# A fused adaptive feed-forward kernel on one core: the last tile's mean taken from the matmuls as a product with the weights' row sums, with the weights kept in rows of 528 elements

## The chip, the cores and the metric

The kernel runs on one core of a Trainium2 chip. The metric is device time in microseconds (us) of one execution, the median over runs of the same kernel. The engines are TensorE (PE; its weight loads are PEld), VectorE (DVE), ScalarE (ACT), GpSimd (POOL) and SyncE (SP), which issues most DMAs. Each runs its own list of instructions in order, and they wait for one another by semaphores.

## The reference

64 sequences of 32 tokens with 512 features, all float32. A small network turns each sequence's condition into a 32 x 32 mixing matrix and a bias; the mixed tokens go through a feed-forward network with a shared and a routed part, whose sum is normalised over the features and added to x.

```python
h = einsum('boi,bih->boh', agg_w, x) + agg_b[:, :, None]      # agg_w, agg_b from the condition
logits = h @ gate_w;  w = top_k(logits, 2)[0].sum(-1)
shared = relu(h @ up_w) ** 2 @ down_w                          # 512 -> 1024 -> 512
routed = ((h @ fc1_w) @ expert_w) * w @ fc2_w                  # 512 -> 256 -> 256 -> 512
y = shared + routed
out = x + (y - y.mean(-1)) * rsqrt(y.var(-1) + 1e-5) * gamma + beta
```

## The kernel before

The 2048 tokens are 16 tiles of 128 tokens, four tiles to a block, so there are four blocks: block 0 is written out, blocks 1 and 2 are one loop body, block 3 is written out. Products are made in float32 precision from operands split into a high and a low part (`down_hi`, `down_lo`, ...): `three_products` issues high x high, high x low and low x high, three matmuls with one destination in PSUM. The expert matrix is folded into fc2 ahead of time, which gives `q` (256 x 512).

In a block TensorE runs the up product (eight chunks `m` of 128 columns of up_w, twelve matmuls each, in four PSUM banks that are reused in turn), the latent and gate products, the mixing for the next block, and the down product. The down product goes tile by tile: six matmuls with `q`, 24 with `down`, each with 512 columns. The bank for up chunk m is free when ScalarE's relu of chunk m - 4 has read it (`relu_done`), and that relu waits until VectorE has split chunk m - 2 (`sq_lo_ready`), because `relu_sq` has two buffers. In the down product tile t waits for VectorE's first sum of tile t - 2 (`y_done`).

VectorE's `normalise(b, t)` adds the two products, takes statistics (L714, L717), adds epsilon (L719), subtracts the mean and multiplies by gamma (L721), waits for GpSimd's `rstd` (a power of -0.5, L417), and makes the result with `x_beta` (L727), which SP stores. GpSimd computes `x_beta` for the next block (L410) once the last tile of a block is finished, and copies the next mixing tiles (L405) after VectorE's reduction of them (L656). VectorE then splits the squares of the next block (L685 a cast, L687 a subtraction).

The last tile of the last block is different. The routing weight is multiplied into its latents beforehand, so that both products add up in one PSUM group, and its 512 columns are made in two halves of 30 matmuls with 256 columns each, in two banks. `normalise_last` takes statistics of each half (L739), aggregates them (L746), and then makes each half's product with gamma (L749) and result (L757). The epsilon is put into the first half's statistics (L742).

The order of all instructions is the order in the code; nothing reorders them. The rows of `down_hi`, `down_lo`, `q_hi` and `q_lo` are 512 float32 elements (2048 bytes) in each partition, and the matmul operands lie in SBUF one behind the other, each tensor starting at a multiple of 128 bytes.

## Time and profile before

| | |
|---|---|
| median of 3 runs | 256.64 us |
| the 3 runs | 256.37, 256.64, 646.71 us |
| profiled execution: span from first to last instruction | 254.6 us |
| median less the span | 2.0 us |
| TensorE busy, granted clock (mean) | 97%, 0.995 |
| VectorE, ScalarE, GpSimd busy | 61%, 32%, 15% |
| chain that ended last | TensorE 89%, DMA 3%, issue 2% |
| last matmul's end to the end of the span | 249.62 to 254.6 us |

The profiled execution's own device time is not listed apart from its span; the 2.0 us stand for what lies around the span. The busy shares are averages over the whole span. Which engine sets the time is read from the chain and from the timeline of each stage: where TensorE is without a gap, what other engines do costs nothing, and after its last matmul every microsecond on the chain of the others is paid.

### The profile page before, as it was taken

Reading aid. Unit: us, or ns where it says so; the run is one execution under the profiler, and the core shown is the slowest. Engines: PE = TensorE matmul, PEld = TensorE weight load, DVE = VectorE, ACT = ScalarE, POOL = GpSimd, SP = SyncE. Lnnn points to the kernel's source line nnn. Section 1 sums busy time; section 2 is a strip of 40 time slices with the busy share of each in tenths; the row PEclk is TensorE's granted clock in tenths of the full one; section 3 lists DMA queues with packets and bytes.
Section 4 is the critical chain, followed back from the end, with each engine's and each line's share of the span. In section 5 each row is a group of like instructions: output and inputs, shape, how many; then the busy total and the mean of one; then the engine's idle time right before and its main releaser. Section 6 shows DMA issues by size and latency. Waiting matters only on the chain.

```text
span 254.6 us, 3526 instructions
## 1 busy us (share of the span) xinstructions
PE 248.0 (97%) x1291; PEld 207.1 (81%) x1291; DVE 155.8 (61%) x272; ACT 81.8 (32%) x142; POOL 39.4 (15%) x45
## 2 busy tenths in 40 slices
PE   8999999999999999999999999999999999999992
PEld 7877887988888888888888888888888888788891
DVE  4798999944448964644447983464444953406453
ACT  4669856411003452321112534331111355202100
POOL 2400021000117120001114411001111700001110
PEclk9999999999999999999999999999999999999997
DMA  6994804001111400001111220000011100000111
GB/s 161 332 324 153 305 17 153 0 0 44 41 41 41 167 0 0 3 0 42 41 41 41 78 87 0 0 0 11 31 41 44 42 0 0 0 3 8 74 44 41
DMA packets 10444, 15.60 MB, mean 61 GB/s; under 512 B 1088, under 2 KB 4928, under 8 KB 10432
## 3 DMA queue, kind: packets, MB, share of 16 engines
q1 hardware_dynamic: 9984, 15.33, 17.6%
q8 instruction: 8, 0.13, 0.2%
q10 hardware_dynamic: 448, 0.11, 0.2%
q14 instruction: 4, 0.03, 0.0%
HBM read 11.23 MB, written 4.20 MB: 61 GB/s over the span
## 4 chain that ended last, share of the span: by engine, by line
PE 89%; DMA 3%; issue 2%; DVE 1%; SPq 1%; ACT 0%; POOL 0%; POOLq 0%; DVEq 0%
PE ps L932 27%; PE ps L934 27%; PE ps L933 27%; PE ps L906 4%; DMA late<-in_up_w_dram 3%; PE ps L998 2%; PE ps L950 1%; PE ps L956 1%; PE ps L952 1%; SPq L322 0%; POOL rstd L417 0%; DVE stats L714 0%; DVE y_buf L712 0%; DVE h_full L636 0%; ACT h_hi L474 0%
## 5 line engine op out<-in xcount | busy, mean ns | idle before, releaser
L932 PE MATMUL ps<-down_hi,sq_hi 128*128 128x512 f32 (+1 forms) x136 | 51.2, 377 | 0.0
L933 PE MATMUL ps<-down_lo,sq_hi 128*128 128x512 f32 (+1 forms) x136 | 51.2, 377 | 0.0
L934 PE MATMUL ps<-down_hi,sq_lo 128*128 128x512 f32 (+1 forms) x136 | 51.2, 376 | 0.0
L932 PE MATMUL ps<-h_hi,up_hi 128*128 128x512 f32 x120 | 46.8, 390 | 0.0
L934 PE MATMUL ps<-h_hi,up_lo 128*128 128x512 f32 x120 | 46.7, 389 | 0.0
L933 PE MATMUL ps<-h_lo,up_hi 128*128 128x512 f32 x120 | 46.7, 389 | 0.0
L417 POOL TENSOR_TENSOR rstd<-mv,half 128x1 f32<-128x1 f32 x16 | 15.3, 954 | 158.2 <-DVE mv L719 153.2
L512 ACT ACTIVATE relu_sq<-ps 128x512 f32<-128x512 f32 x32 | 19.1, 597 | 57.7 <-PE ps L934 44.3
L712 DVE TENSOR_TENSOR y_buf<-ps,y_buf 128x512 f32<-128x512 f32 x15 | 10.4, 692 | 41.0 <-PE ps L934 40.7
L685 DVE CAST sq_hi<-relu_sq 128x512 fp32r<-128x512 f32 x32 | 22.6, 706 | 16.2 <-ACT relu_sq L514 15.7
L932 PEld LDWEIGHTS ps<-down_hi,sq_hi 128*128 128x128 f32 x136 | 25.6, 188 | 4.7
L933 PEld LDWEIGHTS ps<-down_lo,sq_hi 128*128 128x128 f32 x136 | 25.6, 188 | 4.7
L934 PEld LDWEIGHTS ps<-down_hi,sq_lo 128*128 128x128 f32 x136 | 25.6, 188 | 4.7
L529 ACT ACTIVATE y_buf<-ps,top 128x512 f32<-128x512 f32 x15 | 10.2, 687 | 56.7 <-PE ps L934 56.7
L687 DVE TENSOR_TENSOR sq_lo<-relu_sq,sq_hi 128x512 fp32r<-128x512 f32 x32 | 26.5, 828 | 1.1
L932 PEld LDWEIGHTS ps<-h_hi,up_hi 128*128 128x128 f32 x120 | 22.5, 188 | 5.0 <-DVE up_lo L619 0.4
L934 PEld LDWEIGHTS ps<-h_hi,up_lo 128*128 128x128 f32 x120 | 22.5, 188 | 4.7
L933 PEld LDWEIGHTS ps<-h_lo,up_hi 128*128 128x128 f32 x120 | 22.5, 188 | 4.6
L514 ACT ACTIVATE relu_sq<-relu_sq 128x512 f32<-128x512 f32 x32 | 20.2, 632 | 1.0
L727 DVE SCALAR_TENSOR_TENSOR late<-y_buf,rstd,late 128x512 f32<-128x512 f32 x15 | 11.3, 752 | 7.6 <-POOL rstd L417 5.6
L410 POOL TENSOR_TENSOR late<-x_cur,affine_sb 128x2048 f32<-128x2048 f32 x3 | 14.2, 4750 | 2.8 <-DVE late L727 2.8
L932 PE MATMUL ps<-q_hi,lat_hi 128*128 128x512 f32 (+1 forms) x34 | 13.3, 390 | 0.0
(137 smaller groups left out, 308.7 us busy)
## 6 DMA issues: line engine op xcount, KB each, us to landing
out_dram<-late SPq DMA_DIRECT2D x15, 256.0 KB, 2.0
x_cur<-in_x_dram SPq DMA_DIRECT2D x3, 1024.0 KB, 5.2
late<-in_down_w_dram SPq DMA_DIRECT2D x4, 512.0 KB, 5.3
late<-in_up_w_dram SPq DMA_DIRECT2D x3, 512.0 KB, 8.8
x_cur<-in_x_dram SPq DMA_DIRECT2D x2, 512.0 KB, 7.2
experts_sb<-in_experts_dram SPq DMA_DIRECT2D x3, 256.0 KB, 3.5
agg_b<-aggb_dram SPq DMA_DIRECT2D x1, 768.0 KB, 4.9
latents_sb<-in_latents_dram SPq DMA_DIRECT2D x1, 528.0 KB, 4.8
```

Of the source, the lines that this page charges most:

```text
L410: nc.gpsimd.tensor_tensor(x_beta, x_cur[:, :, :], beta_b.unsqueeze(1).to_broadcast([P, TB, HID]), ALU.add).then_inc(xbeta_ready, 1)
L417: nc.gpsimd.tensor_tensor(rstd[:, :], mv[:, 1:2], half[:, :], ALU.pow).then_inc(rstd_done, 1)
L512: nc.scalar.activation(relu_sq[:, m % 2, :], ps[:, UP_BANK[m], :], ACT.Relu).then_inc(relu_done, 1)
L514: nc.scalar.activation(relu_sq[:, m % 2, :], relu_sq[:, m % 2, :], ACT.Square).then_inc(square_done, 1)
L529: nc.scalar.mul(y_buf[:, t % 2, :], routed(t), top2[:, t:t + 1]).then_inc(scaled_done, 1)
L685: nc.vector.tensor_copy(sq_hi[:, m, :], relu_sq[:, m % 2, :]).then_inc(sq_hi_ready, 1)
L687: nc.vector.tensor_tensor(sq_lo[:, m, :], relu_sq[:, m % 2, :], sq_hi[:, m, :].bitcast(fp32), ALU.subtract).then_inc(sq_lo_ready, 1)
L712: nc.vector.tensor_tensor(y, shared(t), y, ALU.add).then_inc(y_done, 1)
L727: nc.vector.scalar_tensor_tensor(out=out_buf[:, t, :], in0=y, scalar=rstd[:, :], in1=x_beta[:, t, :], op0=ALU.mult, op1=ALU.add).then_inc( ...
L932: nc.tensor.matmul(dst, a_hi, b_hi, start=first, stop=False)
L933: nc.tensor.matmul(dst, a_hi, b_lo, start=False, stop=False)
L934: return nc.tensor.matmul(dst, a_lo, b_hi, start=False, stop=last)
```

## The change

The normalisation's mean of a token is the sum of its 512 outputs over 512, and that sum is the product of the token's activations with the row sums of the weights. So two equal columns (512 and 513) are added behind the 512 of `down_hi`, `down_lo`, `q_hi` and `q_lo`; they hold the rows' sums, split in high and low. Rows become 528 elements long (2112 bytes). The sums are made once by VectorE, between the normalisations of block 0's tiles: one reduction behind tile 0, one behind tile 1, and two behind tile 2 with five small instructions that add the parts and split them. In the last tile, the half with columns 256 to 511 is now made first, with columns 512 and 513 after it in the same matmuls (258 columns), so column 256 of its PSUM bank holds the tile's sum when it is done. `normalise_last` divides it by 512 (`last_mean`) and makes the first half's product with gamma while TensorE works at the second half. The other half's product follows the aggregation and no longer waits for its mean. TensorE's last tile waits for `sums_ready`. SP stores the halves in the new order.

```diff
 
         up_hi = sb("up_hi", [P, HC, INT], f32r)
         up_lo = sb("up_lo", [P, HC, INT], f32r)
-        down_hi = sb("down_hi", [P, IC, HID], f32r)
-        down_lo = sb("down_lo", [P, IC, HID], f32r)
+        down_hi = sb("down_hi", [P, IC, HID + PAD], f32r)
+        down_lo = sb("down_lo", [P, IC, HID + PAD], f32r)
         fc1_hi = sb("fc1_hi", [P, HC, LAT], f32r)
         fc1_lo = sb("fc1_lo", [P, HC, LAT], f32r)
-        q_hi = sb("q_hi", [P, LC, HID], f32r)
-        q_lo = sb("q_lo", [P, LC, HID], f32r)
+        q_hi = sb("q_hi", [P, LC, HID + PAD], f32r)
+        q_lo = sb("q_lo", [P, LC, HID + PAD], f32r)
 
 
         h_hi = sb("h_hi", [P, HC, TOK], f32r)
...
         ones = sq_lo[:, 1, 0:P]
         half = sb("half", [P, 1])
         warm = sb("warm", [P, 1])
+        row_sums = sb("row_sums", [P, 2, IC + LC])
+        last_mean = sb("last_mean", [P, 1])
 
         ps = ctx.enter_context(nc.psum_tensor("ps", [P, 8, TOK], fp32))
         H1 = ps[:, 4, 0:2 * NB].rearrange("p (a b) -> p a b", a=2)
...
         def routed(t):
             return ps[:, 6 + t % 2, :]
 
+        LAST_COLS = [slice(HID // 2, HID + 2), slice(0, HID // 2)]
+
         def last_shared(half):
 
             return [shared(TB - 1), ps[:, LAT_BANK[0], :]][half][:, 0:HID // 2]
+
+        LAST_MEAN = shared(TB - 1)[:, HID // 2:HID // 2 + 1]
 
 
         mlp_loaded = [sem(f"mlp_loaded{i}") for i in range(2)]
...
                 store_block(b)
             store_block(NBLK - 1, TB - 1)
             for half in (0, 1):
-                cols = slice(half * HID // 2, (half + 1) * HID // 2)
+                cols = [slice(HID // 2, HID), slice(0, HID // 2)][half]
                 sp.wait_ge(final_done, NT + half)
                 sp.dma_start(out_v[:, NT - 1:NT, cols], out_buf[:, TB - 1:TB, cols]).then_inc(stored[TB - 1], 16)
             for t in range(TB - 1):
...
             def down_high(i):
                 ks = slice(i * DNC, (i + 1) * DNC)
                 act.wait_ge(down_loaded[i], 16)
-                nc.scalar.copy(down_hi[:, ks, :], down_raw[:, ks, :]).then_inc(down_hi_ready, 1)
+                nc.scalar.copy(down_hi[:, ks, 0:HID], down_raw[:, ks, :]).then_inc(down_hi_ready, 1)
 
             for m in range(IC):
                 relu_square(0, m)
...
                                                in1=x_beta[:, t, :], op0=ALU.mult,
                                                op1=ALU.add).then_inc(final_done, 1)
 
+            def sum_rows(weights, at, n, part):
+                nc.vector.tensor_reduce(row_sums[:, part, at:at + n], weights[:, :, 0:HID].bitcast(fp32), AX.X,
+                                        ALU.add).then_inc([hi_summed, lo_summed][part], 1)
+
+            def split_sums():
+                dve.wait_ge(hi_summed, 2)
+                dve.wait_ge(lo_summed, 2)
+                nc.vector.tensor_tensor(row_sums[:, 0, :], row_sums[:, 0, :], row_sums[:, 1, :], ALU.add
+                                        ).then_inc(rows_summed, 1)
+                dve.wait_ge(rows_summed, 1)
+                nc.vector.tensor_copy(down_hi[:, :, HID:HID + 2], row_sums[:, 0, 0:IC].unsqueeze(2).to_broadcast([P, IC, 2])
+                                      ).then_inc(sum_hi_ready, 1)
+                nc.vector.tensor_copy(q_hi[:, :, HID:HID + 2], row_sums[:, 0, IC:IC + LC].unsqueeze(2).to_broadcast([P, LC, 2])
+                                      ).then_inc(sum_hi_ready, 1)
+                dve.wait_ge(sum_hi_ready, 2)
+                nc.vector.tensor_tensor(down_lo[:, :, HID:HID + 2], row_sums[:, 0, 0:IC].unsqueeze(2).to_broadcast([P, IC, 2]),
+                                        down_hi[:, :, HID:HID + 2].bitcast(fp32), ALU.subtract).then_inc(sums_ready, 1)
+                nc.vector.tensor_tensor(q_lo[:, :, HID:HID + 2], row_sums[:, 0, IC:IC + LC].unsqueeze(2).to_broadcast([P, LC, 2]),
+                                        q_hi[:, :, HID:HID + 2].bitcast(fp32), ALU.subtract).then_inc(sums_ready, 2)
+
             def normalise_last():
 
                 b, t = NBLK - 1, TB - 1
                 n = NT
                 y = y_buf[:, t % 2, :]
-                halves = [slice(0, HID // 2), slice(HID // 2, HID)]
+                halves = [slice(HID // 2, HID), slice(0, HID // 2)]
+
+                def times_gamma(i):
+                    cols = halves[i]
+                    nc.vector.scalar_tensor_tensor(out=y[:, cols], in0=last_shared(i), scalar=last_mean[:, :],
+                                                   in1=gamma_b[:, cols], op0=ALU.subtract,
+                                                   op1=ALU.mult).then_inc(gamma_done, 1)
+
                 for i, cols in enumerate(halves):
                     dve.wait_ge(shared_done, n + i)
                     nc.vector.bn_stats(out=last_stats[:, i, :], in_=last_shared(i)).then_inc(stats_done, 1)
...
                         dve.wait_ge(stats_done, n)
                         nc.vector.tensor_scalar(last_stats[:, 0, 2:3], last_stats[:, 0, 2:3], HID * EPS, None,
                                                 ALU.add).then_inc(eps_added, 1)
+                        nc.vector.tensor_scalar(last_mean[:, :], LAST_MEAN, 1.0 / HID, None,
+                                                ALU.mult).then_inc(last_mean_ready, 1)
+                        dve.wait_ge(last_mean_ready, 1)
+                        times_gamma(0)
                 dve.wait_ge(eps_added, 1)
                 dve.wait_ge(stats_done, n + 1)
                 nc.vector.bn_aggr(out=mv[:, :], in_=last_stats[:, :, :]).then_inc(mv_done, 2)
-                dve.wait_ge(mv_done, 2 * n)
-                for i, cols in enumerate(halves):
-                    nc.vector.scalar_tensor_tensor(out=y[:, cols], in0=last_shared(i), scalar=mv[:, 0:1],
-                                                   in1=gamma_b[:, cols], op0=ALU.subtract,
-                                                   op1=ALU.mult).then_inc(gamma_done, 1)
+                times_gamma(1)
                 dve.wait_ge(gamma_done, n + 1)
                 dve.wait_ge(rstd_done, n)
                 dve.wait_ge(xbeta_ready, b + 1)
...
             mix_bias(1, 3)
             mix_low(1, 2)
             mix_low(1, 3)
-            for t in range(TB):
-                normalise(0, t)
+            normalise(0, 0)
+            sum_rows(down_hi, 0, IC, 0)
+            normalise(0, 1)
+            sum_rows(down_lo, 0, IC, 1)
+            normalise(0, 2)
+            sum_rows(q_hi, IC, LC, 0)
+            sum_rows(q_lo, IC, LC, 1)
+            split_sums()
+            normalise(0, 3)
             with dve.Fori(1, NBLK - 1) as b:
                 for m in range(IC):
                     split_square(b, m)
...
                         pe.wait_ge(h_ready, HC * b + 3)
                     if last_block and t == TB - 1:
                         pe.wait_ge(last_lo_ready, LC)
+                        pe.wait_ge(sums_ready, 3)
                         for half in (0, 1):
-                            cols = slice(half * HID // 2, (half + 1) * HID // 2)
+                            cols = LAST_COLS[half]
+                            dst = [shared(TB - 1)[:, 0:HID // 2 + 2], last_shared(1)][half]
                             for lc in range(LC):
-                                three_products(last_shared(half), lat_hi[:, lc, rows], lat_lo[:, lc, rows],
+                                three_products(dst, lat_hi[:, lc, rows], lat_lo[:, lc, rows],
                                                q_hi[:, lc, cols], q_lo[:, lc, cols], lc == 0, False)
                             for m in range(IC):
-                                last = three_products(last_shared(half), sq_hi[:, m, rows], sq_lo[:, m, rows],
+                                last = three_products(dst, sq_hi[:, m, rows], sq_lo[:, m, rows],
                                                       down_hi[:, m, cols], down_lo[:, m, cols],
                                                       False, m == IC - 1)
                             last.then_inc(shared_done, 1)
...
                             pe.wait_ge(lat_hi_ready, LC * b + lc + 1)
                             pe.wait_ge(lat_lo_ready, LC * b + lc + 1)
                         last = three_products(routed(t), lat_hi[:, lc, rows], lat_lo[:, lc, rows],
-                                              q_hi[:, lc, :], q_lo[:, lc, :], lc == 0, lc == LC - 1)
+                                              q_hi[:, lc, 0:HID], q_lo[:, lc, 0:HID], lc == 0, lc == LC - 1)
                     last.then_inc(routed_done, 1)
                     for m in range(IC):
                         if t == 0:
```

The parts left out are the new semaphores and the same `0:HID` in other places that write or read these tensors.

VectorE, block 0, before: the end of tile 2's normalisation and the start of tile 3's. `late` holds the results and `x_beta`.

```order
L727 SCALAR_TENSOR_TENSOR late<-y_buf,rstd,late 128x512
L712 TENSOR_TENSOR y_buf<-ps,y_buf 128x512
L714 BN_STATS stats<-y_buf 128x6
L717 BN_AGGR mv<-stats 128x2
L719 TENSOR_SCALAR mv<-mv 128x1
```

VectorE at the same place now, from the end of tile 2's normalisation on:

```order
L740 SCALAR_TENSOR_TENSOR late<-y_buf,rstd,late 128x512
L745 TENSOR_REDUCE row_sums<-q_hi 128x2
L745 TENSOR_REDUCE row_sums<-q_lo 128x2
L751 TENSOR_TENSOR row_sums<-row_sums 128x10
L754 CAST down_hi<-row_sums 128x8x2
L756 CAST q_hi<-row_sums 128x2x2
L759 TENSOR_TENSOR down_lo<-row_sums,down_hi 128x8x2
L761 TENSOR_TENSOR q_lo<-row_sums,q_hi 128x2x2
L725 TENSOR_TENSOR y_buf<-ps,y_buf 128x512
L727 BN_STATS stats<-y_buf 128x6
```

Two reductions, a sum, two casts and two subtractions stand between tiles 2 and 3. Between tiles 0 and 1 and between tiles 1 and 2 stands one reduction of `down_hi` and of `down_lo` (eight rows of 512 elements each to 128x8).

VectorE, the last tile, before; `last_stats` are the statistics, `y_buf` the product with gamma, `late` the result:

```order
L739 BN_STATS last_stats<-ps 128x6
L742 TENSOR_SCALAR last_stats<-last_stats 128x1
L739 BN_STATS last_stats<-ps 128x6
L746 BN_AGGR mv<-last_stats 128x2
L749 SCALAR_TENSOR_TENSOR y_buf<-ps,mv,affine_sb 128x256 x2
L757 SCALAR_TENSOR_TENSOR late<-y_buf,rstd,late 128x256 x2
```

and now:

```order
L779 BN_STATS last_stats<-ps 128x6
L782 TENSOR_SCALAR last_stats<-last_stats 128x1
L784 TENSOR_SCALAR last_mean<-ps 128x1
L773 SCALAR_TENSOR_TENSOR y_buf<-ps,last_mean,affine_sb 128x256
L779 BN_STATS last_stats<-ps 128x6
L790 BN_AGGR mv<-last_stats 128x2
L773 SCALAR_TENSOR_TENSOR y_buf<-ps,last_mean,affine_sb 128x256
L797 SCALAR_TENSOR_TENSOR late<-y_buf,rstd,late 128x256 x2
```

One product with gamma has moved ahead of the second half's statistics, with a one-element scaling of the sum ahead of it; one has stayed behind the aggregation.

TensorE, the step from tile 2 of the last block to the first half of the last tile, before:

```order
L934 MATMUL ps<-down_hi,sq_lo 128x512
L932 MATMUL ps<-q_hi,lat_hi 128x256
L933 MATMUL ps<-q_lo,lat_hi 128x256
L934 MATMUL ps<-q_hi,lat_lo 128x256
L932 MATMUL ps<-q_hi,lat_hi 128x256
```

and now:

```order
L981 MATMUL ps<-down_hi,sq_lo 128x512
L979 MATMUL ps<-q_hi,lat_hi 128x258
L980 MATMUL ps<-q_lo,lat_hi 128x258
L981 MATMUL ps<-q_hi,lat_lo 128x258
L979 MATMUL ps<-q_hi,lat_hi 128x258
```

The 30 matmuls of this half have 258 columns for 256; the second half's 30 keep 256. The number of instructions on TensorE is the same.

## Rows read from the trace of the kernel before

**Rows 1.** The page: busy times (1) and the granted clock in 40 slices (2)

```profile
PE 248.0 (97%) x1291; PEld 207.1 (81%) x1291; DVE 155.8 (61%) x272; ACT 81.8 (32%) x142; POOL 39.4 (15%) x45
...
PEclk9999999999999999999999999999999999999997
```

**Rows 2.** Timeline, TensorE, last tile: start us, length us, line, operation, count

```profile
242.27 0.28 PE L932 MATMUL ps<-q_hi,lat_hi 128*128 128x256 f32 x1
...
249.34 0.28 PE L934 MATMUL ps<-down_hi,sq_lo 128*128 128x256 f32 x1
```

**Rows 3.** Table by stretch, one tile of block 0: stretch, its length, busy (count)

```profile
54.73:61.53 6.80, 6.80 (x32) 5.63 (x31) 3.14 (x7) 0.69 (x1) 0.92 (x1) 1.00 0.11 41
```

**Rows 4.** Timeline, VectorE, the end of the program

```profile
246.26 0.43 DVE L739 BATCH_NORM_STATS2 last_stats<-ps 128x6 f32<-128x256 f32 x1
...
249.66 0.43 DVE L739 BATCH_NORM_STATS2 last_stats<-ps 128x6 f32<-128x256 f32 x1 [2.79 <-PE ps L934]
250.22 0.21 DVE L746 BATCH_NORM_AGGREGATE mv<-last_stats 128x2 f32<-128x12 f32 x1
250.47 0.88 DVE L749 SCALAR_TENSOR_TENSOR y_buf<-ps,mv,affine_sb 128x256 f32<-128x256 f32 x2
251.38 0.88 DVE L757 SCALAR_TENSOR_TENSOR late<-y_buf,rstd,late 128x256 f32<-128x256 f32 x2
```

**Rows 5.** Timeline, GpSimd, the end of the program

```profile
250.51 0.55 POOL L417 TENSOR_TENSOR rstd<-mv,half 128x1 f32<-128x1 f32 x1 [5.01 <-DVE mv L746]
```

**Rows 6.** Timeline, VectorE and GpSimd, an ordinary tile of the last block

```profile
232.45 0.74 DVE L721 SCALAR_TENSOR_TENSOR y_buf<-y_buf,mv,affine_sb 128x512 f32<-128x512 f32 x1
...
232.61 0.98 POOL L417 TENSOR_TENSOR rstd<-mv,half 128x1 f32<-128x1 f32 x1 [30.26 <-DVE mv L719]
...
233.69 0.75 DVE L727 SCALAR_TENSOR_TENSOR late<-y_buf,rstd,late 128x512 f32<-128x512 f32 x1 [0.49 <-POOL rstd L417]
```

**Rows 7.** Groups by shape, VectorE: count, busy us, mean ns, idle before

```profile
L719 DVE TENSOR_SCALAR mv<-mv 128x1 f32<-128x1 f32 x15 | 2.3, 154 | 0.8 <-DVE mv L717 0.3
...
L612 DVE TENSOR_REDUCE agg<-relu_sq 128x64 f32<-128x512 f32 x2 | 1.4, 686 | 0.1
...
L749 DVE SCALAR_TENSOR_TENSOR y_buf<-ps,mv,affine_sb 128x256 f32<-128x256 f32 x2 | 0.9, 480 | 0.0
```

**Rows 8.** One line, the reduction of 1024 elements: ns min/median/max

```profile
L656 DVE TENSOR_REDUCE agg<-y_buf x3: 1210/1214/1214, 26.9 to 150.2; 128x1024 f32 x2, 128x128 f32<-128x1024 f32 x1
```

**Rows 9.** Timeline, VectorE, last tile of block 0

```profile
75.13 0.69 DVE L712 TENSOR_TENSOR y_buf<-ps,y_buf 128x512 f32<-128x512 f32 x1 [3.00 <-PE ps L934]
...
78.18 0.75 DVE L727 SCALAR_TENSOR_TENSOR late<-y_buf,rstd,late 128x512 f32<-128x512 f32 x1 [0.49 <-DVE y_buf L721]
```

**Rows 10.** Timelines, block 1: GpSimd, VectorE, ScalarE, TensorE

```profile
79.01 4.66 POOL L410 TENSOR_TENSOR late<-x_cur,affine_sb 128x2048 f32<-128x2048 f32 x1 [0.92 <-DVE late L727]
...
94.14 0.29 POOL L405 COPY mix<-agg 32x128 f32 x1 [0.16 <-POOL mix L405]
...
79.07 4.88 DVE L685 CAST sq_hi<-relu_sq 128x512 fp32r<-128x512 f32 x1
83.99 0.69 DVE L687 TENSOR_TENSOR sq_lo<-relu_sq,sq_hi 128x512 fp32r<-128x512 f32 x1
84.60 0.42 DVE L685 CAST sq_hi<-relu_sq 128x512 fp32r<-128x512 f32 x1
...
84.77 0.60 ACT L512 ACTIVATE relu_sq<-ps 128x512 f32<-128x512 f32 x1 [3.01 <-DVE sq_lo L687]
...
91.18 0.39 PE L932 MATMUL ps<-h_hi,up_hi 128*128 128x512 f32 x1
...
103.14 1.05 PE L906 MATMUL ps<-mix,x_cur 128*128 128x128 f32 x7
```

**Rows 11.** DMA issues: count, KB each, median us to landing

```profile
x_cur<-in_x_dram SPq DMA_DIRECT2D x3, 1024.0 KB, 5.2
...
out_dram<-late SPq DMA_DIRECT2D x2, 128.0 KB, 1.8
```

More of the change, by code:

```diff
@@ L58, in adaln_ffn_kernel @@
     WB = 4
+    PAD = 16
     UP_COLS = [(0, 1), (1, 1), (2, 2), (4, 2), (6, 2)]
@@ L305, in adaln_ffn_kernel @@
         gamma_done = sem("gamma_done")
+        hi_summed = sem("hi_summed")
+        lo_summed = sem("lo_summed")
+        rows_summed = sem("rows_summed")
+        sum_hi_ready = sem("sum_hi_ready")
+        sums_ready = sem("sums_ready")
+        last_mean_ready = sem("last_mean_ready")
         final_done = sem("final_done")
@@ L464, in q_high @@
                 act.wait_ge(q_done, lc + 1)
-                nc.scalar.copy(q_hi[:, lc, :], Q[lc]).then_inc(q_hi_ready, 1)
+                nc.scalar.copy(q_hi[:, lc, 0:HID], Q[lc]).then_inc(q_hi_ready, 1)
             def mix_high(b):
@@ L623, in q_low @@
                 dve.wait_ge(q_hi_ready, lc + 1)
-                nc.vector.tensor_tensor(q_lo[:, lc, :], Q[lc], q_hi[:, lc, :].bitcast(fp32),
+                nc.vector.tensor_tensor(q_lo[:, lc, 0:HID], Q[lc], q_hi[:, lc, 0:HID].bitcast(fp32),
                                         ALU.subtract).then_inc(q_lo_ready, 1)
@@ L763, in down_low @@
                 dve.wait_ge(down_hi_ready, i + 1)
-                nc.vector.tensor_tensor(down_lo[:, ks, :], down_raw[:, ks, :], down_hi[:, ks, :].bitcast(fp32),
+                nc.vector.tensor_tensor(down_lo[:, ks, 0:HID], down_raw[:, ks, :], down_hi[:, ks, 0:HID].bitcast(fp32),
                                         ALU.subtract).then_inc(down_lo_ready, 1)
@@ L1036, in down_product @@
                         last = three_products(shared(t), sq_hi[:, m, rows], sq_lo[:, m, rows],
-                                              down_hi[:, m, :], down_lo[:, m, :], m == 0, m == IC - 1)
+                                              down_hi[:, m, 0:HID], down_lo[:, m, 0:HID], m == 0, m == IC - 1)
                     last.then_inc(shared_done, 1)
```

## The prediction

> **What bounds the kernel now.** I read the page's busy times and slices first. TensorE is busy in 97% of the span, at full clock in 39 of 40 slices [rows 1]; the span is 254.6 us. So up to the last matmul only something that makes TensorE wait, or makes its matmuls longer, can move the time; VectorE (61% busy), ScalarE and GpSimd work beside it. The second view is the timeline of the end. TensorE's last matmul starts at 249.34 and ends at 249.62 [rows 2]; the remaining 5.0 us hold no matmul, and there the chain runs through VectorE, GpSimd and the store. The reader is to see, in [rows 4]: statistics of the second half at 249.66, aggregation 250.22 to 250.43, the two products with gamma from 250.47 (0.88 together, 0.48 each as [rows 7] record them), the two final products from 251.38. GpSimd's inverse deviation runs 250.51 to 251.06, inside the products with gamma, and the stores of the two halves land 1.8 us after their issue [rows 11].
>
> **The sum is made against the profiled execution** (254.6 us span). The median, 256.64, lies 2.0 us above it, and I take these 2.0 us as unchanged.
>
> **Part 1, the end (the gain).** Before, both products with gamma need the mean of the aggregation and stand between it and the final products. Now the first half's product runs right after the first half's statistics: its input is ready when TensorE has ended the first half (242.27 + 29 x 0.1198 = 245.74, and 0.28 for the last one: 246.02), VectorE takes its statistics at 246.26 [rows 2, 4]. Added there: one 1-element scaling (0.15, as L719 [rows 7]), a wait on it (a few hundredths), one product of 0.48 [rows 7]. With the epsilon step VectorE is free by some 247.7, and the second half's statistics start at 249.66 [rows 4]: 2 us of cover, cost nothing. If that cover were gone, every microsecond would be paid in full.
> Behind the aggregation one product is left: 250.43 + 0.02 + 0.48 = 250.93. The final product also waits for GpSimd's result. That ends at 250.51 + 0.55 = 251.06 [rows 5], and in an ordinary tile VectorE starts 0.10 after GpSimd ends (232.61 + 0.98 = 233.59, start at 233.69) [rows 6]. So the final products start at 251.16, no longer at 251.38: **gain 0.22 us**, and the path that is late next is aggregation, GpSimd, final product. The removal of 0.40 to 0.44 from VectorE is worth only half of itself. Both finals and both stores keep their order and sizes (columns 256 to 511 now come first) and shift with it.
> Bounds: GpSimd's duration is the soft row. It is 0.98 in ordinary tiles, where VectorE's product reads two SBUF tensors beside it [rows 6], and 0.55 in the last tile, where that product reads PSUM and one SBUF tensor [rows 4, 5]. The remaining product still reads PSUM, so I take 0.55. If the true duration were 0.85, the gain would be nothing; 0.98 would put the start at 251.59, a loss of 0.21. If the semaphore came at once, the start would be VectorE's 250.97, a gain of 0.4.
>
> **Part 2, two more columns.** The 30 matmuls of the first half write 258 columns in place of 256. A 512-column matmul takes 6.80 / 30 = 0.2267 us [rows 3], a 256-column one (249.34 - 242.27) / 59 = 0.1198 [rows 2]; the slope is 0.417 ns a column, and 30 x 2 x 0.417 = **0.025 us**, on the path. No matmul is added.
>
> **Part 3, the row sums in block 0.** VectorE gets four reductions and five small instructions between the normalisations of the first block's tiles. A reduction of 512 elements takes 0.686 us [rows 7], of 1024 elements 1.214, the middle of three [rows 8], so 4096 elements take 1.214 + 3072 x 1.031 ns = 4.38 us: two of these, two of 1.21, and five small ones of about 0.15 to 0.17 with three waits, 1.05 together. Sum 12.2 us. A normalisation takes 3.80 us (75.13 to 78.18 + 0.75 = 78.93) out of a tile's 6.80 [rows 3, 9], so three gaps of 3.0 us cover 9 of it. The first one starts three tiles before the last, at 75.13 - 20.40 = 54.73, and ends at 58.53. Laid out in order: reduction 58.57 to 62.95; tile 1's normalisation to 66.79 (without the change 65.33); reduction to 71.21; tile 2 to 75.05; the two short reductions to 77.5; the splitting to 78.55; tile 3 ends at 82.4 instead of 78.93. VectorE leaves block 0 **3.5 us late**.
> Who waits for that? TensorE's tile 3 waits for tile 1's first sum, now at 63.7, and tile 3 starts near 68.1, 0.2 before tile 2's normalisation would: no stall. ScalarE scales tile 3 once tile 1 is finished (66.8) and its six routed matmuls are through (68.1 + 6 x 0.2267 = 69.5): no stall. GpSimd's x + beta waits for tile 3 and moves from 79.01 to 82.5; VectorE's first cast of block 1 (4.88 us long) and its subtraction (83.99 to 84.68) move along, so does ScalarE's third relu, which waits for that subtraction, from 84.77 to 88.3, ending at 88.9 [rows 10]. TensorE needs that relu's bank for the seventh up product, whose first matmul starts at 91.18 [rows 10], its weights a little earlier: **2.1 us of slack remain**. Behind it VectorE needs 1.1 us for each chunk (0.42 + 0.69) against TensorE's 2.72 (12 x 0.2267), so the delay is worked off by the end of the up products. On SP's queue the load of the next x goes out 3.5 us later and takes 5.2 [rows 11], so it is there by 93; on GpSimd the last copy of the next mix tiles (94.14 to 94.43) moves back by 3.5 at most, to 97.9; TensorE reads both from 103.14 on [rows 10]. Cost nothing.
> The row shows the first cast of block 1 at 4.88 us where the next one takes 0.42, beside GpSimd's 4.66 us addition [rows 10], and I let the whole delay pass through it. The Trainium skill (SBUF — State Buffer, section "SBUF: two separate sides") says that VectorE and GpSimd share one port pair, which one instruction holds to its end while the other blocks. The trace agrees with it (4.88 against 4.66). Without that lock the cast would run at 82.5 and the slack would be near 6.5 us in place of 2.1; the sum is the same by both.
>
> **Part 4, rows of 528 elements.** Before, the rows of down and q are 2048 bytes apart and all start at multiples of 128 bytes; now they are 2112 apart, so every second one (odd m, odd lc) starts 64 bytes past such a multiple. ScalarE's and VectorE's splitting of the weights now writes broken rows instead of one run, in block 0's up phase, where TensorE does not wait. TensorE reads these rows in all 510 matmuls of the down phases. I take zero change: the change keeps multiples of 64. No row of the trace shows a matmul of this type at such an offset, so this price is the open one. From below zero: a matmul already takes 0.2267 us where 512 columns at 2.4 GHz, one a cycle, need 0.2133, so at most those 13.3 ns could go, and nothing in an offset would take them away. From above I use the same 13.3 ns, paid a second time.
>
> **Sum**: -0.22 + 0.025 = -0.20 us, span 254.4, time 256.64 - 0.20 = **256.4 us**.
>
> **The rivals.**
> (a) The end gains nothing: GpSimd's result, not VectorE's product, was what the final product would have waited for. For it: its spans are rough, and beside an ordinary tile's product it lasts 0.98 [rows 6]. Against it: the final product at 251.38 waited for nothing more, so GpSimd's result was there by then. Between 0.55 and 0.98 this gives 256.4 to 256.9; I call it 256.7. It is also the case in which the change does not do what it says, since the mean no longer holds anything up but the deviation does.
> (b) Slower by the row offset: 13.3 ns on the 255 matmuls with odd rows is 3.4 us, 259.8; on all 510 it is 6.8 us, 263.2. It passes 2% (5.1 us) from 10 ns on each of the 510. Against it: nothing in the trace speaks for a dependence on the offset; for it only that no row excludes it.
> (c) Slower by the reductions: should they run at half the speed that [rows 7, 8] show, VectorE is 11.2 us later still; less the slack of 2.1 TensorE stalls 9.1 us at the seventh up product of block 1: 265.5. It costs from 2.1 us of further delay on, and passes 2% from 7.2 us. Against it: three recorded reductions of 1024 elements agree to 4 ns [rows 8], and the new ones read longer unbroken runs than those.
> The Trainium skill (VectorE: DVE Perf Modes, section "The perf-mode tier table") says that a reduction has only the one-element-a-cycle mode. The recorded 1.03 ns an element agrees.
>
> **How the numbers follow.** Forecast 0.70; (a) 0.19; (b) 0.06, half of it beyond 2%; (c) 0.04, mostly beyond 2%; 0.01 for something else at the end. 2% either way is about what a measurement of this kernel can tell from no change, and the whole effect I forecast is 0.08%. So: slower by over 2% 0.06, within 2% 0.93, faster by over 2% 0.01, since even the whole 5.0 us after the last matmul are less than 2%. The range: forecast and (a) hold 0.89 and span 256.2 to 256.9; executions of the kernel before differ by 0.27 us, so 255.9 to 257.2, and a ns or so on each matmul of part 4 lifts the upper end to 257.3. The single reading of 646.71 is left out.
>
> **What would show it.** Right: 30 matmuls of 258 columns about 0.1206 apart; 512-column ones of both down and up still 0.2267 apart; reductions of 4.4, 4.4, 1.2 and 1.2 us; the long cast near 82.5; no idle time of TensorE at 91; a product with gamma before 248, one behind the aggregation, and the first final product starting 1.54 us after the last matmul's end in place of 1.76, with GpSimd as what ended its wait. Wrong: matmuls of the down phases farther apart than those of the up phases (b), a stall of TensorE in block 1 (c), GpSimd's last span near 1 us (a).

## The result, and the profile after

The changed kernel takes 259.01 us (median of 5, 258.75 to 259.21) against 256.37 of the kernel before on the same chip (a reading of 646.71 left out): ratio 1.0094, 95% interval 1.0073 to 1.0115. It is 2.6 us slower; the prediction was 256.4 with 257.3 as its upper end.

The lines below are the span, the busy times and the granted clock from the page of the kernel after; [rows 1] has those of before. The span has grown from 254.6 to 257.1, TensorE's busy time by 2.8, and the clock is full.

```profile
span 257.1 us, 3537 instructions
...
PE 250.8 (98%) x1291; PEld 207.5 (81%) x1291; DVE 166.9 (65%) x282; ACT 81.9 (32%) x142; POOL 39.1 (15%) x45
...
PEclk9999999999999999999999999999999999999999
```

More busy time with the same number of instructions means longer matmuls, not a stall. The groups by line and shape on TensorE (count, busy us, mean ns) say which: those that read `down`, not those that read `h`.

```profile
L980 PE MATMUL ps<-down_lo,sq_hi 128*128 128x512 f32 x120 | 47.5, 396 | 0.0
L979 PE MATMUL ps<-down_hi,sq_hi 128*128 128x512 f32 x120 | 47.4, 395 | 0.0
L981 PE MATMUL ps<-down_hi,sq_lo 128*128 128x512 f32 x120 | 47.2, 393 | 0.0
L979 PE MATMUL ps<-h_hi,up_hi 128*128 128x512 f32 x120 | 46.8, 390 | 0.0
```

Before, all such groups had a mean of 389 or 390. These means contain the overlap of neighbours (a matmul is shown as 0.39 us long, while the next one starts after 0.23), so the clean measure is the distance from one start to the next. ScalarE scales each tile once, behind the tile's sixth matmul. Its timeline in block 0, after:

```profile
50.88 0.69 ACT L542 ACTIVATE y_buf<-ps,top 128x512 f32<-128x512 f32 x1
56.49 0.69 ACT L542 ACTIVATE y_buf<-ps,top 128x512 f32<-128x512 f32 x1 [4.93 <-PE ps L981]
63.47 0.69 ACT L542 ACTIVATE y_buf<-ps,top 128x512 f32<-128x512 f32 x1 [6.29 <-PE ps L981]
70.44 0.69 ACT L542 ACTIVATE y_buf<-ps,top 128x512 f32<-128x512 f32 x1 [6.29 <-PE ps L981]
```

and before:

```profile
50.60 0.68 ACT L529 ACTIVATE y_buf<-ps,top 128x512 f32<-128x512 f32 x1
56.02 0.69 ACT L529 ACTIVATE y_buf<-ps,top 128x512 f32<-128x512 f32 x1 [4.73 <-PE ps L934]
62.82 0.69 ACT L529 ACTIVATE y_buf<-ps,top 128x512 f32<-128x512 f32 x1 [6.11 <-PE ps L934]
69.62 0.69 ACT L529 ACTIVATE y_buf<-ps,top 128x512 f32<-128x512 f32 x1 [6.11 <-PE ps L934]
```

A tile of 30 matmuls takes 6.97 us in place of 6.80 [rows 3]: 232.5 ns a matmul, 5.8 more. Fifteen full tiles give 15 x 0.173 = 2.6 us. As a sum over the whole kernel: from that first scaling to the last tile's first matmul it is 245.15 - 50.88 = 194.27 us after, and 242.27 - 50.60 = 191.67 before, 2.60 apart.

TensorE in the last tile, after, beside [rows 2]:

```profile
245.15 0.28 PE L979 MATMUL ps<-q_hi,lat_hi 128*128 128x258 f32 x1
...
248.75 0.28 PE L979 MATMUL ps<-q_hi,lat_hi 128*128 128x256 f32 x1
...
252.13 0.28 PE L981 MATMUL ps<-down_hi,sq_lo 128*128 128x256 f32 x1
```

30 matmuls of 258 columns at 0.1200 us, then 29 distances of 0.1166, where before each took 0.1198: this tile has become 0.09 us shorter. Behind it, VectorE and GpSimd, beside [rows 4, 5]:

```profile
249.14 0.42 DVE L779 BATCH_NORM_STATS2 last_stats<-ps 128x6 f32<-128x256 f32 x1
...
249.67 0.15 DVE L784 TENSOR_SCALAR last_mean<-ps 128x1 f32<-128x1 f32 x1
...
249.85 0.48 DVE L773 SCALAR_TENSOR_TENSOR y_buf<-ps,last_mean,affine_sb 128x256 f32<-128x256 f32 x1
...
253.01 0.21 DVE L790 BATCH_NORM_AGGREGATE mv<-last_stats 128x2 f32<-128x12 f32 x1
253.14 0.43 DVE L773 SCALAR_TENSOR_TENSOR y_buf<-ps,last_mean,affine_sb 128x256 f32<-128x256 f32 x1
253.94 0.88 DVE L797 SCALAR_TENSOR_TENSOR late<-y_buf,rstd,late 128x256 f32<-128x256 f32 x2 [0.37 <-POOL rstd L430]
...
253.30 0.55 POOL L430 TENSOR_TENSOR rstd<-mv,half 128x1 f32<-128x1 f32 x1 [4.92 <-DVE mv L790]
```

The last matmul ends at 252.13 + 0.28 = 252.41, the final products start 1.53 later (before 1.76), and what they wait for is GpSimd: 0.23 us gained.

VectorE in block 0 and at the start of block 1, after, beside [rows 9, 10]:

```profile
58.90 4.41 DVE L745 TENSOR_REDUCE row_sums<-down_hi 128x8 f32<-128x4096 f32 x1
...
66.94 4.41 DVE L745 TENSOR_REDUCE row_sums<-down_lo 128x8 f32<-128x4096 f32 x1
...
74.98 1.21 DVE L745 TENSOR_REDUCE row_sums<-q_hi 128x2 f32<-128x1024 f32 x1
76.11 1.21 DVE L745 TENSOR_REDUCE row_sums<-q_lo 128x2 f32<-128x1024 f32 x1
...
81.11 0.75 DVE L740 SCALAR_TENSOR_TENSOR late<-y_buf,rstd,late 128x512 f32<-128x512 f32 x1 [0.49 <-DVE y_buf L734]
81.78 0.42 DVE L698 CAST sq_hi<-relu_sq 128x512 fp32r<-128x512 f32 x1
82.23 5.03 DVE L700 TENSOR_TENSOR sq_lo<-relu_sq,sq_hi 128x512 fp32r<-128x512 f32 x1
```

The sums cost TensorE nothing: its busy share in the table by stretch of that block is the whole stretch.

```profile
56.24:63.22 6.98, 6.98 (x31) 5.64 (x31) 6.34 (x6) 0.69 (x1) 0.92 (x1) 1.00 0.11 40
63.22:70.19 6.97, 6.97 (x31) 5.64 (x31) 6.30 (x8) 0.69 (x1) 0.99 (x1) 1.00 0.10 38
```

So the profile accounts for the span: +2.60 in fifteen tiles, -0.09 in the last, -0.23 behind it, and +0.28 that is there already at the first scaling (50.88 for 50.60); sum 2.56, measured 2.5. The +0.28 looks like scatter of the beginning, which no run settles: run 5 below, which changes no relation between operands, has 50.84 there, and the kernel with rows of 576 has 50.56.

### The profile page after: what moved, and what is told of

Its sections match the earlier page's. It is cut to its first block, busy times and chain, and to the rows that moved or that the text cites. A ratio compares the mean times of both kernels' runs of the same rounds, so it can differ in the third digit from the quotient of the medians.

```text
span 257.1 us, 3537 instructions
## 1 busy us (share of the span) xinstructions
PE 250.8 (98%) x1291; PEld 207.5 (81%) x1291; DVE 166.9 (65%) x282; ACT 81.9 (32%) x142; POOL 39.1 (15%) x45
## 4 chain that ended last, share of the span: by engine, by line
PE 93%; issue 2%; DVE 1%; ACT 1%; POOL 1%; POOLq 0%; DVEq 0%; ACTq 0%
PE ps L979 27%; PE ps L980 27%; PE ps L981 27%; PE ps L953 4%; PE ps L1045 2%; PE ps L900 1%; PE ps L959 1%; PE ps L906 1%; PE ps L997 1%; PE ps L1003 1%; PE ps L999 1%; POOL rstd L430 0%; PE ps L925 0%; DVE stats L727 0%; DVE h_full L649 0%
## 5 line engine op out<-in xcount | busy, mean ns | idle before, releaser
L980 PE MATMUL ps<-down_lo,sq_hi 128*128 128x512 f32 (+2 forms) x136 | 52.0, 382 | 0.0
L979 PE MATMUL ps<-down_hi,sq_hi 128*128 128x512 f32 (+2 forms) x136 | 51.9, 382 | 0.0
L981 PE MATMUL ps<-down_hi,sq_lo 128*128 128x512 f32 (+2 forms) x136 | 51.7, 380 | 0.0
L979 PE MATMUL ps<-q_hi,lat_hi 128*128 128x512 f32 (+2 forms) x34 | 13.3, 391 | 0.0
```

What stands on the lines that cost most here:

```text
L979: nc.tensor.matmul(dst, a_hi, b_hi, start=first, stop=False)
L980: nc.tensor.matmul(dst, a_hi, b_lo, start=False, stop=False)
L981: return nc.tensor.matmul(dst, a_lo, b_hi, start=False, stop=last)
```

## The experiments

A word that the rest needs. A matmul has a **moving** operand, whose row of 512 elements streams through (in the down phase a row of `down` or `q`, in the up and latent phases a row of `h`), and **weights**, here the 128 x 128 operand that TensorE holds meanwhile (`sq`, `lat` in the down phase; `up`, `fc1` in the others), not the network's weights. The **offset** below is the byte address of the moving row's start less that of the weights' start, modulo 256, from the addresses that the kernel's tensors are given. Before, all of these tensors start 128 past a multiple of 256 and their rows are multiples of 256 bytes long: the offset is 0 everywhere. With rows of 2112 bytes it is 64 x m in the down phase, so it runs through 0, 64, 128, 192. In each run the distances of up and latent matmuls are read from TensorE's timeline of block 1 (first and last start of a phase over the count), those of the down phase from the tiles' distance over 30, which takes in the six matmuls with `q`. Starts are given to 0.01 us, so a figure from the 23 distances of a latent phase is good to some 0.4 ns.

**1. Rows of 528 alone.** The kernel before, with nothing of the sums, the last tile or its order.

```diff
-        down_hi = sb("down_hi", [P, IC, HID], f32r)
+        down_hi = sb("down_hi", [P, IC, HID + PAD], f32r)     # PAD = 16; down_lo, q_hi, q_lo too
```

> The kernel before with rows of 528 elements for down and q, and nothing else of the change. If the addresses of the rows lengthen the matmuls of the down phases, their mean distance goes from 226.7 to about 232.4 ns here as in the changed kernel, on 510 matmuls: +2.5 to +2.9 us, about 259.1. If something else of the change does it (the reductions, the two columns, the order of the halves), this kernel takes 256.4 and all its 512-column matmuls stay 226.7 ns apart.

259.09 us (258.69 to 259.22), ratio 1.0102 [1.0085, 1.0118]; tiles at 56.33, 63.31, 70.28. The whole loss is there without the sums.

**2. The sums alone.** The kernel before, with the reductions and the splitting in block 0, written to tensors of their own that nothing reads; rows stay 512.

```diff
+        sum_hi = sb("sum_hi", [P, IC + LC, 2], f32r)          # and sum_lo
-            for t in range(TB):
-                normalise(0, t)
+            normalise(0, 0)
+            sum_rows(down_hi, 0, IC, 0)
...
```

> The kernel before, rows of 512, with the reductions and the splitting of the row sums added at the same places in block 0, their results in tensors of their own that nothing reads. If the delay of VectorE in block 0 is hidden as the trace of the changed kernel suggests, the time is that of before, 256.4, within 0.2. If VectorE's long reads are what disturbs the matmuls, it goes up towards 259, with longer distances in block 0 alone or in all blocks.

256.82 us (256.44 to 257.14, 10 runs), ratio 1.0018 [1.0008, 1.0028]. Its profiled run has a span of 254.2, and up, latent and down matmuls at 226.7, as before. So the reductions don't stall TensorE. The median is nevertheless 0.46 above that of the kernel before, and this lies outside the span: the spans have a median of 254.55 us over the 10 runs and of 254.5 over the 13 of the kernel before, while the time around the span is 2.17 to 2.33 us in all 10 and 1.76 to 1.86 in all 13. Why it is longer in this kernel stays open; run 8, with the same reductions, has 1.81 to 1.94.

**3. The rows left at 2048 bytes, their start moved by 64.** This was to tell a price of broken rows from one of position.

```diff
+        gap_down_hi = sb("gap_down_hi", [P, 16])              # ahead of down_hi: 64 bytes
+        gap_h_hi = sb("gap_h_hi", [P, 16])                    # ahead of h_hi: 64 more
```

> The kernel before, rows of 512, with 64 bytes left free ahead of down_hi and again ahead of h_hi: down, fc1 and q start 64 bytes past a multiple of 128, everything from h_hi on 128 bytes later than before. If a moving row that starts 64 bytes past a multiple of 128 costs by itself, all 510 matmuls of the down phases get longer, by 5 ns or more each (+2.5 us or more). If what counts is a change of offset from one moving operand to the next, nothing gets longer (256.4). If what counts is the offset of the moving row against that of the weights loaded beside it, the latent products (64 apart), the up products (128 apart) and the down products (64 apart the other way) each move by an amount of their own, constant inside each group; shorter is as possible as longer.

261.18 us (260.87 to 261.4), ratio 1.0182 [1.0165, 1.0199]. Rows are unbroken and it is slower still. The groups by shape show that the up products, which nothing had touched before, are longer now as well:

```profile
L934 PE MATMUL ps<-down_hi,sq_hi 128*128 128x512 f32 x120 | 47.4, 395 | 0.0
...
L934 PE MATMUL ps<-h_hi,up_hi 128*128 128x512 f32 x120 | 47.4, 395 | 0.0
```

Two gaps had moved three relations: up 128 (232.5 ns), latent 64 (229.1), down 192 (7.00 us a tile, 233.3 ns). The next runs separate a tensor's own address from its relation to the weights.

**4. The low parts of down and q 64 bytes on, all else as before.**

```diff
+        gap_down_lo = sb("gap_down_lo", [P, 16])              # and 192 bytes ahead of fc1_hi
+        gap_q_lo = sb("gap_q_lo", [P, 16])                    # and 192 bytes ahead of h_hi
```

> The kernel before, rows of 512, with down_lo and q_lo 64 bytes further than down_hi and q_hi against the multiples of 256; up, h, fc1, sq and lat keep their places modulo 256. If a change of offset between successive moving operands costs, two of every three matmuls of the down phases get longer (hi to lo, lo to hi), the third (hi to hi) stays at 226.7 ns. If a row's own offset costs, one of three gets longer. If the offset between moving row and weights counts, the pairs around the low part change, two of three, by the amount that the shift of 64 shows in the other run.

258.53 us (258.42 to 258.82), ratio 1.0084 [1.0067, 1.0101]; 6.96 us a tile, up still 226.6. One product in three has an offset, and the tile pays 5.3 ns a matmul on average over all three. The timeline shows it on each of them alike, so matmuls at offset 0 are delayed too when a neighbour has an offset.

**5. Everything 64 bytes on together** (a gap ahead of `up_hi`, the first of them): every address is changed and no relation.

> The kernel before, rows of 512, every tensor 64 bytes later, so that all matmul operands start 192 bytes past a multiple of 256 in place of 128, and none changes against another. If the offset of the moving row against the weights counts, all 512-column matmuls stay 226.7 ns apart and the time is 256.4. If the address by itself counts (a start 64 bytes past a multiple of 128), about 960 matmuls of 512 columns get some 6 ns longer: 262.

256.63 us (256.18 to 256.95, 10 runs), ratio 0.9997 [0.9979, 1.0014], 6.80 a tile. That all operands lie 64 bytes further costs nothing; so what the other runs paid for was a change of their relation.

**6 and 7. Weights and h moved, not the down rows.** In the sixth `down` and its rows stay where they were and `sq` moves; in the seventh three other offsets are set.

```diff
+        gap_fc1_hi = sb("gap_fc1_hi", [P, 16])                # 6: 64 bytes; 7: 32
+        gap_h_hi = sb("gap_h_hi", [P, 32])                    # 6: 128 bytes; 7: 32
+        gap_sq_hi = sb("gap_sq_hi", [P, 16])                  # 7 only: 64 bytes
```

> The kernel before, rows of 512, tensors moved so that, modulo 256, the moving rows stand against the weights at +192 bytes (up), +128 (latent), +64 (down) and +128 (q with lat). By the relative offset: up products as the down products of the run with a shift of 64 (233.3 ns), latent and q products as its up products (233), down products as its latent products (between 226 and 230). By the address of the moving row alone: down products, which stay at 128, keep 226.7 ns, and only the up and latent products get longer, equally.

> The kernel before, rows of 512, tensors moved so that, modulo 256, the moving rows stand against the weights at +64 (up), +32 (latent), +128 (down) and +160 (q with lat). By the relative offset: up products as the latent ones of the run with a shift of 64 (226 to 230 ns), down products 233; the offset of 32 tells whether anything finer than 64 shows. By the address of the moving row alone the down products keep 226.7.

The sixth: 260.8 us (2 runs), ratio 1.0168 [1.015, 1.0185]; up 233.3 ns, latent 232.2, down 6.89 us a tile, 0.09 more than before. In it the `down` rows are those of the kernel before to the byte, and the 24 matmuls that read them start 229.0 ns apart for 226.7 (the other six read `q`, which is 64 bytes on and at offset 128). The seventh: 260.64 us (2 runs), 1.0161 [1.0144, 1.0179]; up 229.0, latent 233.5, down 6.98 a tile.

**8. The changed kernel with rows of 576** (2304 bytes, 9 x 256): the whole change is kept and every offset is 0. To make room, nine small tensors that only the beginning uses are laid into the unused part of `agg_b`.

```diff
-    PAD = 16
+    PAD = 64
+        early = agg_b[:, TOK:]
-        mlp_sb = sb("mlp_sb", [D, mlp.shape[1]])
+        mlp_sb = early[0:D, 0:mlp.shape[1]]                   # and eight more
```

> The changed kernel with rows of 576 elements (2304 bytes, a multiple of 256) in place of 528, so that all moving rows and weights stand at 128 modulo 256; small tensors that are used only at the start lie in a part of agg_b that is filled later, to make room. If the offsets were the whole loss, all 512-column matmuls are 226.7 ns apart again and the rest of the change shows: the end 0.2 us shorter, so 256.2 to 256.7 (the sums alone measured 256.8 against 256.4). If anything else of the change costs, it stays above 257.5.

256.30 us (12 runs, 256.13 to 256.74 and one of 258.62) against 256.50 of the kernel before (23 runs, with one of 258.69), ratio 1.0002 [0.9986, 1.0018]: the loss is gone. It isn't the move of the nine tensors that does it, since run 10 has it too and keeps the loss. ScalarE's tiles, VectorE and GpSimd at the end:

```profile
55.97 0.69 ACT L543 ACTIVATE y_buf<-ps,top 128x512 f32<-128x512 f32 x1 [4.73 <-PE ps L982]
62.77 0.69 ACT L543 ACTIVATE y_buf<-ps,top 128x512 f32<-128x512 f32 x1 [6.11 <-PE ps L982]
```

```profile
249.30 0.28 PE L982 MATMUL ps<-down_hi,sq_lo 128*128 128x256 f32 x1
...
251.11 0.88 DVE L798 SCALAR_TENSOR_TENSOR late<-y_buf,rstd,late 128x256 f32<-128x256 f32 x2 [0.37 <-POOL rstd L431]
```

The final products start 1.53 us after the last matmul's end (249.58), as in the changed kernel: span 254.3 for 254.6. A gain of 0.2 us is what the profile shows and what the prediction's sum came to. The medians of the spans agree with it (254.45 over the 12 runs, 254.7 over the 23 of before), but the interval of the ratio can't tell it from none.

**9. The changed kernel with rows of 514** (2056 bytes), with gaps so that each tensor starts where it did before, modulo 256: the rows are at no multiple of 64.

> The changed kernel with rows of 514 elements (2056 bytes, no padding behind the two columns) and spacers so that each tensor still begins 128 bytes past a multiple of 256; the moving rows then stand 8 bytes apart modulo 256 from row to row. If only the offset against the weights counts, the down phases get longer by an amount for offsets of 0 to 56 bytes, the up and latent products stay at 226.7 ns. If operands off the multiples of 64 bytes cost more than the changed kernel's, the down phases' mean distance lies above 232.5 ns and the time above 259.2; if small offsets are cheap, below.

259.1 us (258.82 to 259.38), ratio 1.0108 [1.0088, 1.0128]; 6.99 a tile. Rows at multiples of 64 bytes (6.97) are only 0.02 us a tile better than rows that are not.

**10. Rows of 544** (2176 bytes): offsets 0 and 128 in turn.

> The changed kernel with rows of 544 elements (2176 bytes, a multiple of 128 but not of 256), the start's small tensors lying in agg_b. The moving rows stand at 0 (even m) or 128 bytes (odd m) against the weights modulo 256. If 256 bytes is the period that counts, the odd rows cost 6 ns as the up products did at 128, some 229.5 ns on average in the down phases, about 257.7. If multiples of 128 bytes are enough, 226.7 ns and 256.3.

258.83 us (258.33 to 259.18), ratio 1.0095 [1.0072, 1.0118]; 6.96 a tile. I had expected the mean of the two; the three matmuls of a row at offset 0 between rows at 128 are no shorter than the rest (in the tile that starts at 114.61 us the three of such a row take 0.70 or 0.71 us together, those of a row at 128 take 0.69 or 0.70).

**11. Offsets of 8 to 32 bytes**, in the kernel before: `h` 16 bytes on, `fc1` and `sq` 32, `lat` 8, so up has +16, latent -16, down -32 (and `q` -8).

```diff
-        sq_hi = sb("sq_hi", [P, IC, TOK], f32r)
+        sq_hi = sb_at("sq_hi", [P, IC, TOK], f32r, 8)         # starts 8 elements into its place
```

> The kernel before, rows of 512, with operands moved by less than 64 bytes: the moving rows stand at +16 bytes (up), -16 (latent), -32 (down) and -8 (q with lat) against the weights. If the distance of 226.7 ns is a valley at exactly 0, all four groups get longer, by up to 6 ns. If some small offset is better than 0, a group falls below 226.7; 213.3 is what 512 columns at the full clock would leave.

261.4 us (2 runs), ratio 1.0197 [1.0173, 1.0222]: up 231.7 ns, latent 236.5, down 6.98 a tile. Already 16 bytes on either side of 0 cost 5 and 10 ns, more than 64 bytes did.

**12. Rows of 576 and the last tile cut at column 240.** In run 3 the last tile's matmuls of 256 columns at offset 192 had been shorter (113.7 ns) than at 0 (119.8). Here the first part, columns 240 to 513, has offset 192 and the second, columns 0 to 239, has 0.

```diff
-        LAST_COLS = [slice(HID // 2, HID + 2), slice(0, HID // 2)]
+        CUT = 240
+        LAST_COLS = [slice(CUT, HID + 2), slice(0, CUT)]
```

> The changed kernel with rows of 576 elements and the last tile cut at column 240 in place of 256, so that its first part (272 columns and the two sums) starts 192 bytes past a multiple of 256 against the weights and its second part (240 columns) at 0; all other matmuls stay at 0. If the gain that 256-column matmuls showed at 192 (113.3 for 120.0 ns in the run with a shift of 64) holds for 274, that part takes about 120 ns a matmul, and the second some 113: the last tile is 0.2 us shorter than with rows of 576 alone and the three small steps on 240 columns some 0.05: about 256.1, a ratio just under 1 against before. If a cut off the 256 bytes only brings the loss of other offsets, the part with 274 columns takes 127 ns or more and the time is that of rows of 576, 256.3, or above.

256.3 us (255.95 to 256.6, 12 runs), ratio 0.999 [0.9981, 0.9998] against 256.52. TensorE's last tile:

```profile
242.36 0.29 PE L981 MATMUL ps<-q_hi,lat_hi 128*128 128x274 f32 x1
...
246.17 0.27 PE L981 MATMUL ps<-q_hi,lat_hi 128*128 128x240 f32 x1
...
249.41 0.27 PE L983 MATMUL ps<-down_hi,sq_lo 128*128 128x240 f32 x1
```

274 columns take 127.0 ns each, not the 120 that I expected (119.8 and 18 columns more at the prediction's 0.417 ns make 127.3, so offset 192 brings nothing here); 240 take 111.7; the tile takes 7.05 us for 7.07. It is 0.1% below the kernel before, and nearly all of that is the shorter end. Whether it is faster than rows of 576 alone isn't shown: both medians are 256.3 us, on different chips.

The offset and the distance of starts, for matmuls of 512 columns in block 1 (down: the 24 matmuls with `down` alone, over all 15 tiles):

| offset | kernel, phase | ns a matmul |
|---|---|---|
| 0 | before, all; 5, all; 8, all | 226.7 |
| +16, -16, -32 | 11: up, latent, down | 231.7, 236.5, 233.4 |
| 32 | 7: latent | 233.5 |
| 64 | 3: latent; 6: down; 7: up | 229.1, 229.0, 229.0 |
| 128 | 3: up; 6: latent; 7: down | 232.5, 232.2, 232.5 |
| 192 | 3: down; 6: up | 233.1, 233.3 |
| mixed, mean of a tile | after; 4; 9; 10 | 232.5, 232.0, 233.0, 232.0 |

The offset isn't all of it. Run 11 has the same latent product, with the same operands at the same addresses, in block 0 and in block 1:

```profile
37.62 0.39 PE L937 MATMUL ps<-h_hi,fc_hi 128*128 128x512 f32 x1
...
42.84 0.39 PE L939 MATMUL ps<-h_hi,fc_lo 128*128 128x512 f32 x1
...
98.00 0.40 PE L937 MATMUL ps<-h_hi,fc_hi 128*128 128x512 f32 x1
...
103.44 0.40 PE L939 MATMUL ps<-h_hi,fc_lo 128*128 128x512 f32 x1
```

These are 24 matmuls each: 5.22 / 23 = 227.0 ns apart in block 0, as at offset 0, and 5.44 / 23 = 236.5 in block 1. In run 3 the same phase (offset 64) has 233.0 in block 0 and 229.1 in block 1. And the kernel before, with offset 0 everywhere, has longer distances behind a wait in its first up product:

```profile
20.97 0.50 PE L932 MATMUL ps<-h_hi,up_hi 128*128 128x512 f32 x1
21.30 0.40 PE L933 MATMUL ps<-h_lo,up_hi 128*128 128x512 f32 x1
...
23.39 0.39 PE L933 MATMUL ps<-h_lo,up_hi 128*128 128x512 f32 x1
```

The nine distances from 21.30 to 23.39 have a mean of 232.2 ns; behind them it is 226.7 again. The granted clock is 1.00 in all these stretches. So something besides the offset has a part; it could be what TensorE did just before, or, for the two blocks, the transfers and the other engines' work, which are heavier in block 0. No run separates these.

## Why the prediction was wrong

**Where it failed.** The failed step is Part 4: "I take zero change: the change keeps multiples of 64." The term is not zero but 5.8 ns on each of the 450 matmuls with 512 columns in the down phases, 2.6 us (runs 1 and 8: put in alone it makes the loss, taken out of the change it removes it). A multiple of 64 was no reason at all: run 9, without it, loses the same. What the kernel before has and the change loses is a distance of a multiple of 256 bytes between row and weights, and no row of the trace before could show that it matters, since it has it everywhere. That trace did hold a price, though, which the part didn't use: the nine distances of 232.2 ns shown above. On 450 matmuls these 5.5 ns more make 2.5 us, by an estimate; that both are the same effect isn't shown. I had the case as rival (b) at 0.06, with the right cause in the main (the row offset, in the down phases only; the runs add that it counts against the weights' place) and 13.3 ns as price; measured, it is less than half of that, but on even and odd rows alike. The range ended at 257.3 because it added only 0.1 us for this part. It calls that "a ns or so on each matmul", but a ns on each of 510 is 0.5 us, and the bound that the part itself had named was 3.4 to 6.8.

**Part 1, the end.** Right: 1.54 forecast, 1.53 measured, GpSimd as what ends the wait and 0.55 as its duration [rows 5]. So rival (a) fell: of VectorE's 0.4 only 0.23 came, since GpSimd is late next. One figure of the bounds is off: the gain would be nothing from a GpSimd duration of 0.77 on (250.51 + 0.77 + 0.10 = 251.38), not 0.85.

**Part 2, two more columns.** Right at offset 0: 0.1206 forecast, and run 8 has (245.82 - 242.23) / 30 = 0.1197; two columns are below what the timeline resolves. That the changed kernel comes so near too, with 0.1200, is luck: at the same mixed offsets run 1 has (248.51 - 244.99) / 30 = 0.1173 for this half with 256 columns, so there the two columns cost some 2.7 ns a matmul, on a lower base.

**Part 3, the row sums.** Right: 4.41, 4.41, 1.21 and 1.21 us, forecast 4.38 and 1.21, so rival (c) fell. VectorE leaves the block at 81.86 (forecast 82.4), although the tiles came 0.17 us later each; TensorE doesn't wait. One detail differs: the long instruction of block 1 was to be the cast and is now the subtraction behind it (5.03), beside GpSimd's addition of 4.77. ScalarE's third relu starts at 87.36, not 88.3, before the 91 at which it is needed. By the Trainium skill (SBUF — State Buffer, section "SBUF: two separate sides") the two engines lock each other out of a shared port; that the stall moved to whichever VectorE instruction meets GpSimd's is what it would give, and the trace agrees.

**The sum.** Without Part 4's term it was right: 254.4 forecast as span, 254.3 with rows of 576.

## What to carry to other kernels

Where TensorE sets the time, an edit that changes the row length or the place of a matmul operand is priced by experiment first: one run of the kernel before with only the new row length would have shown the loss, and here padding to the next multiple of 256 bytes kept the old distance at no cost in time. A condition that holds everywhere in a trace can't be tested by it, so a range has to include its bound, not a fraction of it. Look too for a stretch in which the same instruction already runs slower: it gives a first price. When the gain is 0.2 us at the end, compare it with the smallest price that a new cost can have per matmul times their number: here 0.5 ns would have cancelled it.

## What the runs showed of the hardware

In the steady phases of this kernel (block 1) matmuls of 512 columns start every 226.7 ns where the moving row and the weights start a multiple of 256 bytes apart, and every 229.0 to 236.5 at all other offsets tried. A shift of all operands by 64 bytes is without effect (run 5), and matmuls at offset 0 between others don't profit (runs 4 and 10): one product in three at offset 64 brings all to 232.0, more than a constant 64 does (229.0). The offset doesn't fix the distance alone: behind a wait nine matmuls at offset 0 were 232.2 apart in the kernel before, and in run 11 the latent product at -16 ran at 227.0 in block 0. The reductions aren't the reason: run 1 has none of them and loses as much, and in the changed kernel the tiles of block 0, with VectorE reducing, and of block 1, without, are both 6.97 apart.

Short matmuls go the other way. 256 columns take 119.8 ns at offset 0 and less at the others: 113.6 at 192 (run 3), 117.8 to 118.5 over the last tiles of runs 1, 4, 6, 7 and 11, 116.6 in the second half of the changed kernel's last tile, 119.0 in that of run 10. What in the chip makes the distance count was not settled; the runs show where it cost time in this kernel and how much, not why.
